# Two causal attentions of one Trainium2 kernel: from batches of whole heads to units of four heads and half the queries

## The reference, cut to what matters

```python
# layer 0: queries and keys get a bias and a rotation by position
q, k, v = (x @ W + b for each).reshape(16 heads, 16)
# gate of layer 1's feed-forward part: the same without bias and rotation
scores = einsum('bqhd,bkhd->bhqk', q, k) / sqrt(16)
scores = where(k_index <= q_index, scores, -large)
out = softmax(scores) @ v        # then a product with Wo
```

## Time and profile before

| what | us |
|---|---|
| median of three runs | 3222.04 |
| lowest, highest | 3208.08, 3231.48 |
| the profiled execution's own time | 3223.99 |
| its span, first to last instruction | 3222.1 |
| TensorE busy in the span | 2691.4 |
| VectorE busy | 1827.7 |
| GpSimd busy | 1411.9 |
| ScalarE busy | 1229.2 |
| first attention in the span, first transfer to last multiplication | 60.05 to 319.64 |
| second attention, the same | 1580.76 to 1838.22 |
| mean granted TensorE clock, share of full speed | 0.895 |

### The profile page before, as it was taken

The page is one execution under the profiler, slowest core; times in us unless marked ns, Lnnn a source line. Parts: engine busy times, 40 slices in busy tenths (PEclk is TensorE's granted clock), DMA queues, the critical chain, the costliest instruction groups (busy, mean ns, idle before and its releaser), DMA issues. The chain is left out here.

```text
span 3222.1 us, 41641 instructions
## 1 busy us (share of the span) xinstructions
PE 2691.4 (84%) x13826; PEld 1822.3 (57%) x13826; DVE 1827.7 (57%) x2624; ACT 1229.2 (38%) x2035; POOL 1411.9 (44%) x1110
## 2 busy tenths in 40 slices
PE   4888799767999999998588876868787777998798
PEld 3454677543444444445444455756676665776676
DVE  3753355456666666633366233676757576554465
ACT  4355233353555555552345422323232332233222
POOL 2542334364888888882255122313131221343133
PEclk7789899897999999998678888889989987998799
DMA  1310111121111111100121011001000000110011
GB/s 52 49 21 1 39 44 44 41 69 40 34 33 34 27 27 27 27 1 26 29 43 21 7 42 39 24 1 34 0 26 8 21 7 21 34 49 28 21 35 42
DMA packets 47269, 94.03 MB, mean 29 GB/s; under 512 B 11553, under 2 KB 25761, under 8 KB 46497
## 3 DMA queue, kind: packets, MB, share of 16 engines
q1 hardware_dynamic: 44544, 88.53, 11.2%
q10 hardware_dynamic: 2592, 3.82, 0.3%
HBM read 59.81 MB, written 3.15 MB: 20 GB/s over the span
## 5 line engine op out<-in xcount | busy, mean ns | idle before, releaser
L2042 DVE TENSOR_REDUCE a1h_mseg<-bank 128x2 f32<-128x1024 f32 x256 | 302.4, 1222 | 185.2 <-PE bank L1807 177.0
L1969 ACT ACTIVATE a1h_prob<-bank 128x512 f32<-128x512 f32 x440 | 247.3, 598 | 190.8 <-PE bank L1863 105.0
L1791 POOL TENSOR_TENSOR a_qk<-a_qk,a1h_prob 128x512 f32<-128x512 f32 x230 | 298.4, 1332 | 49.1 <-ACT a1h_prob L1969 49.0
L63 POOL TENSOR_TENSOR f_wh<-f_raw,ones_r 128x768 fp32r<-128x768 f32 (+1 forms) x74 | 111.3, 1504 | 406.4 <-PE bank L402 371.9
L391 PE MATMUL bank<-x_norm_h,f_wh 128*128 128x512 f32 x592 | 242.2, 409 | 10.6 <-POOL f_wl L359 10.1
L391 PE MATMUL bank<-x_norm_l,f_wh 128*128 128x512 f32 x592 | 237.4, 401 | 0.0
L391 PE MATMUL bank<-x_norm_h,f_wl 128*128 128x512 f32 x592 | 236.7, 400 | 0.0
L600 DVE SCALAR_TENSOR_TENSOR f_tf<-bank,f_bias,f_sg 128x512 f32<-128x512 f32 x148 | 111.0, 751 | 202.6 <-PE bank L391 181.7
L2425 POOL TENSOR_TENSOR x_norm<-x_norm,l2a_tab 128x512 f32<-128x512 f32 x64 | 87.9, 1381 | 298.0 <-ACT x_norm L2639 247.7
L1876 PE MATMUL bank<-a1h_prob,a_v 128*64 128x512 f32 x880 | 215.0, 603 | 0.0
L1861 PE MATMUL bank<-a1h_ql,a1h_k 128*128 128x512 f32 x512 | 202.0, 395 | 0.0
(11 more groups left out here) (581 smaller groups left out, 6996.8 us busy)
## 6 DMA issues: line engine op xcount, KB each, us to landing
f_raw<-in_l_w_dram SPq DMA_DIRECT2D x66, 385.0 KB, 3.1
a1h_st_q<-a_qk SPq DMA_DIRECT2D x128, 128.0 KB
a_staging<-a_qk SPq DMA_DIRECT2D x384, 32.0 KB
a_qk<-l_keys SPq DMA_DIRECT2D x32, 128.0 KB, 2.7
l2a_vraw<-in_l2a_wvg_dram SPq DMA_DIRECT2D x8, 512.0 KB, 4.1
l2a_qkraw<-in_l2a_wqk_dram SPq DMA_DIRECT2D x32, 128.0 KB, 2.1
f_raw<-in_l_w_dram SPq DMA_DIRECT2D x8, 449.0 KB, 3.4
a1p_raw<-in_l1a_w_dram SPq DMA_DIRECT2D x20, 128.0 KB, 2.0
```

The source lines that it names most:

```text
L63: return pool.tensor_tensor(dst, src, one.to_broadcast(list(src.shape)), ALU.mult)
L1791: pool.tensor_tensor(out, first, slot_of[t % NP], ALU.add).then_inc(sum_done, 1)
L1969: act.activation(slot_of[t % NP], core.bank[2 + t % 3][:, :], ACT.Exp, scale=scale).then_inc(p_ready, 1)
L2042: dve.tensor_reduce(mseg[:, :, qb, s], spare(("A", n, k))[:, :, :], AX.X, ALU.max).then_inc(a_read, 1)
```

## The change

Only the two causal attentions, and what feeds them, are touched. `attend` and `attend_plan` are taken out; `attend_causal` takes their place.

- The work is cut into 8 units: four heads ("quad" Q) and one half h of the queries. A unit of the first half has 4 steps of 128 keys, one of the second half 8, so 48 steps in all. Order: (0,0) (1,0) (0,1) (1,1) (2,0) (3,0) (2,1) (3,1).
- A head's operand has 64 rows: high, low and high parts in 16 rows each, and 16 rows for the maxima. Two heads lie in one 128-row tile; their products are issued side by side in the upper and the lower 64 rows of the array.
- Rows are gathered by transfers of 64 KB, 12 for two heads (96 instead of 192 in all). They read the high and low parts, which are now made once for all heads on the four source chunks, before the gather. ScalarE copies the gathered rows into operands of type fp32r (`rounding`), 16 copies of 128x1024; the first eight stand ahead of all exponentials in its order.
- Maxima: 48 visits of 4 products each, two reductions of 128x2 by up to 1024 columns. Visits run up to 11 ahead of the steps. The maxima of a unit go to rows by 8 fp32 products with a negated identity, and VectorE adds them to the query rows. GpSimd does nothing in the loop.
- Scores go to three banks in turn instead of two. Masks are products of 64 rows by 64 columns, two for each head instead of one of 128x128.
- Values: as before four column tiles, now read straight from `v` (the copies at L1519 go).
- A unit's end works on 512 columns instead of 1024; ScalarE spreads the inverse, and results overwrite the query chunk Q in place.
- The zero and one fills of `a_staging` (second and third fill, L987) go; two fills of 128x2048 are made inside the new block. Weights' order and constants are laid out to match.

```diff
-    HEADS = 8
-    per = 4 if causal else 2
...
+def attend_causal(nc, core, name, qk, v, scale, masks_dram):
+    QUADS = 4
+    UNITS = [(2 * g + b, h) for g in range(2) for h in range(NH) for b in range(2)]
+    KEYS_OF = (4, 8)
+    K = 64
+    NP = 12
+    SLOTS = 3
...
+    def visits_by(g):
+        return min(len(visits), 6 + g + 1 + min(4, max(0, g - 1)))
+    head = [("A", x) for x in range(4)] + [("M", 0)] + [("A", x) for x in range(4, 6)]
...
+    for w in range(len(UNITS)):
+        after[LAST_STEP[w] + 3].append(("D", w))
+        after[LAST_STEP[w] + 5].append(("R", w))
...
+        @block.sync
+            for i in range(2 * QUADS):
+                g, j0 = i // 4, 2 * (i % 4)
+                if i == 0:
+                    sp.wait_ge(filled, 2)
+                for c in range(2):
+                    if i >= 2:
+                        sp.wait_ge(rounded, 2 * (i - 2) + c + 1)
+                    part = ((HI, 0), (HI, 16), (LO, 32)) if c == 0 else ((HI, 0), (HI, 32), (LO, 16))
+                    for src, r in part:
+                        sp.wait_ge(hi if src is HI else lo[g], ...)
+                        for u in range(2):
+                            sp.dma_start(raw[c][64 * u + r:64 * u + r + 16, i % 2, :],
+                                         src[g][j0 + u:P:8, c, :].bitcast(F32)).then_inc(rows_in[i % 2][c], 16)
...
+            def maxima(x):
+                if h == 0 and qb == 0:
+                    pe.wait_ge(rounded, 4 * (Q + 1))
+                for p in range(2):
+                    wait_spare(pe, ("A", x, p))
+                    for u in range(2):
+                        rows = slice(64 * u, 64 * u + K)
+                        mm = pe.matmul(ps[:, u, 0:n], qt[rows, ..., qb * P:(qb + 1) * P],
+                                       kt[rows, ..., s * HALF:s * HALF + n], ..., tile_position=(64 * u, 0))
...
+            def max_rows(w):
+                for i in range(8):
+                    mm = pe.matmul(ps[:, i // 4, (i % 4) * P:(i % 4 + 1) * P], mpos[:, w % 2, i, :], nident[:, :],
+                                   start=True, stop=True)
...
+            def scores(g):
+                for p in range(2):
+                    for u in range(2):
+                        t = 4 * g + 2 * p + u
+                        if t >= 3:
+                            pe.wait_ge(p_ready, t - 2)
+                        mm = pe.matmul(core.bank[2 + t % 3][:, 0:n], kt[...], qt[...], ..., tile_position=(64 * u, 0))
+                    if diag:
+                        for c in range(2):
+                            for u in range(2):
+                                mm = mask(pe, core.bank[2 + t % 3][:, 64 * c:64 * c + 64], 1, c, u)
...
+            def values(g):
+                for b in range(4):
+                    mm = pe.matmul(core.bank[5][32 * b:32 * b + 32, c0:HALF], v[:, kb, 4 * Q + b, :],
+                                   prob[:, (4 * g + b) % NP, 0:n], ..., tile_position=(0, 32 * b))
...
+            for g in range(len(steps) + 6):
+                if g < len(steps):
+                    scores(g)
+                others([e for e in after[g] if e[0] in "AM"])
+                if 0 < g <= len(steps):
+                    values(g - 1)
+                others([e for e in after[g] if e[0] in "DR"])
...
+            high(0)
+            high(1)
+            for i in range(4):
+                for c in range(2):
+                    rounding(i, c)
...
+                    for b in range(4):
+                        act.wait_ge(s_ready, t + 1)
+                        act.activation(prob[:, t % NP, 0:n], core.bank[2 + t % 3][:, 0:n], ACT.Exp, scale=scale)
...
+                    dve.tensor_reduce(mseg[:, w % 2, 2 * p:2 * p + 2, qb % 4, s], spare(("A", x, p))[:, :, 0:n], AX.X,
+                                      ALU.max).then_inc(a_read, 1)
...
 def small_attention(nc, core, name, a, key, on, dst, tables, v_bias, add_x):
-        attend(nc, core, name + "h", qk, 2, None, v, on, 0.25, True, 2, a["spread"], a["causal"], staging=staging)
+        attend_causal(nc, core, name + "h", on, v, 0.25, a["causal"])
```

More of the change, by code:

```diff
@@ new lines, in values @@
+            def values(g):
+                w, kb = steps[g]
+                Q, h = UNITS[w]
+                c0, n, diag = width(g)
+                if kb == 0 and w:
+                    pe.wait_ge(ou_done, w)
+                pe.wait_ge(p_ready, 4 * g + 4)
+                for b in range(4):
+                    mm = pe.matmul(core.bank[5][32 * b:32 * b + 32, c0:HALF], v[:, kb, 4 * Q + b, :],
+                                   prob[:, (4 * g + b) % NP, 0:n], start=kb == 0, stop=kb == KEYS_OF[h] - 1,
+                                   skip_group_check=True, tile_position=(0, 32 * b))
+                mm.then_inc(av_done, 1)
@@ new lines, in sums, with inverse @@
+            def sums(w):
+                wait_spare(pe, ("D", w))
+                pe.wait_ge(ou_done, w + 1)
+                ps = spare(("D", w))
+                for b in range(4):
+                    mm = pe.matmul(ps[:, 0, 4 * b:4 * b + 4], ou[:, w % 2, b * P:(b + 1) * P], pick[:, :], start=True,
+                                   stop=True)
+                mm.then_inc(a_ready, 1)
+            def inverse(w):
+                wait_spare(pe, ("R", w))
+                pe.wait_ge(rx_done, w + 1)
+                ps = spare(("R", w))
+                for b in range(4):
+                    mm = pe.transpose(ps[:, 0, b * P:(b + 1) * P], rx[:, b, :, :].rearrange("p a d -> p (a d)"),
+                                      core.ident[:, :])
+                mm.then_inc(a_ready, 1)
@@ new lines, in others @@
+            def others(events):
+                for kind, x in events:
+                    if kind == "A":
+                        maxima(x)
+                    elif kind == "M":
+                        max_rows(x)
+                    elif kind == "D":
+                        sums(x)
+                    else:
+                        inverse(x)
+            pe.wait_ge(made, 3)
+            others(head)
+            for g in range(len(steps) + 6):
[5 more added lines that the diff above has]
+                others([e for e in after[g] if e[0] in "DR"])
@@ new lines, in scale_products @@
+            def scale_products(w):
+                Q, h = UNITS[w]
+                dve.wait_ge(a_ready, use["R", w] + 1)
+                dve.wait_ge(ou_done, w + 1)
+                dve.tensor_tensor(qk[:, Q, half(h)], ou[:, w % 2, :], spare(("R", w))[:, 0, :],
+                                  ALU.mult).then_inc(on_done, 1)
+            dve.wait_ge(made, 3)
+            for kind, x in head:
+                if kind == "A":
+                    maxima(x)
+                else:
+                    add_maxima(x)
@@ new lines, in _ @@
+            for g in range(len(steps) + 6):
+                for kind, x in [e for e in after[g] if e[0] in "AM"] + [e for e in after[g] if e[0] in "DR"]:
+                    if kind == "A":
+                        maxima(x)
+                    elif kind == "M":
+                        add_maxima(x)
+                    elif kind == "D":
+                        invert(x)
+                    elif kind == "R":
+                        scale_products(x)
+            dve.wait_ge(on_done, len(UNITS))
```

737 lines of the change are left out of this document (205 added, 532 removed).

## The result

| | us |
|---|---|
| forecast (range) | 3169 (3080 to 3240) |
| kernel after, median of four runs | 3270.98 (3258.84 to 3290.16) |
| kernel before, measured beside it | 3224.16 (3208.08 to 3231.48) |
| ratio after/before, with its 95% interval | 1.0144 (1.011 to 1.0178) |
| profiled execution after: time, span, mean clock | 3269.16, 3267.3, 0.869 |

The change made the kernel slower by 1.4%, and the time lies outside the range. What came is close to the price of the third rival ("the clock stays low", 3280), but 20 of the 45 us lie in a block that this rival does not speak of.

The account below looks back on a forecast made before the run. In the attention loops TensorE's stream binds for three batches, the score-to-exponential chain in the last. Gains 2 x (17.5 start + 6.2 loop + 2.1 end) + 1 = 52.6 us give 3171.4, with the lower median 3169 us; range 3080 to 3240.

Parts of the forecast that it names:

- third rival: Attention loops: the clock stays low; at two thirds low the loop takes 244 us, the kernel 3280; chance 0.11.
- Start: Each attention's start: first exponential at 99.7 us, about 40 behind the block's start instead of 57; gain 17.5 us.
- the rival of a gather bound by rate: Attention start: transfers run at 48.7 GB/s, first exponential 15 us later than before, kernel 3235 us; chance 0.09.
- The loop's work: Each attention's loop at full clock: steps, visits, maxima, sums, transposes and waits add up to 178.7 us.
- The chain of a step: Loop: fourth score waits for the first's exponential, since three banks turn; 2.61 us for a full step without visit.
- second rival: Attention loops: two heads' products don't run side by side; 23 us more, 212 with the clock, kernel 3217; chance 0.11.
- The clock: Attention loops: 13% at the low clock, half the old share, makes 178.7 into 188.5 us; gain 6.2.
- The progress at the low clock: Loop at 1.2 GHz: a step with a visit goes from 3.2 to 5.3 us, progress 0.6.
- The prediction's own bounds for the loop: Loop gain: 16 us with no low clock, −49 with two thirds low.
- The first rival: Attention loops: waits overlap better, TensorE's own 122.6 us binds, 131 with low clock; kernel 3055 us; chance 0.25.
- The end: Each attention's end, from last values to multiplication: 5.65 us instead of 7.8, gain 2.1.
- Other stages: Stages outside the two attentions: taken as unmoved; the forecast would be wrong if they move by over 3 us.

Follow-up runs that it names:

- the ninth: Kernel after with four extra 64-row products of 512 columns, two and two side by side, ahead of each visit half: 3256.2 us, ratio 1.011.
- the second experiment: Kernel after with a unit's maxima moved to rows by 8 transposes instead of 8 fp32 products, VectorE subtracting them: 3266.8 us, ratio 1.0145.
- the best kernel: Kernel after with the visit between the score pairs, maxima as transposes and 65 idle TensorE instructions more in each causal attention: 3140.2 us, ratio 0.9745.
- 12: Kernel after with 104 instructions (waits already met) more in TensorE's program of each causal attention: 3265.6 us, ratio 1.0134.
- 13: Kernel after with the visit between the score pairs, maxima as transposes and 97 idle TensorE instructions more in each causal attention: 3157.2 us, ratio 0.9794.
- 15: Kernel after with the visit between the score pairs, maxima as transposes and a padding of 481 TensorE instructions in each causal attention: 3227.3 us, ratio 1.002.
- The third experiment: Kernel after with a step's maxima visit between its two score pairs, or the values of the step before where there is no visit: 3173.5 us, ratio 0.9875.
- the eighth: Kernel after with the visit split, one half behind each pair of scores, then the values: 3196.8 us, ratio 0.9923.
- 17: Kernel after with 76 instructions (waits already met) more in TensorE's program of each causal attention: 3258.7 us, ratio 1.0105.

## Why the prediction was wrong

**Start: right in sum.** Forecast 40 us from block start to first exponential, 40 measured. The price per transfer was 0.62 us where I had 0.67, and the scores behind the copies took 2.0 us that I had at nothing; that the two cancel is luck. The gain was 17 us of the 17.5; the rival of a gather bound by rate is out.

**The loop's work: right within a tenth, on the high side.** Forecast 178.7 us at full clock. By the full-clock stretch TensorE is busy 29.79/36 = 83%, and its work is 135 us, so 163; the ninth's second loop, all at full clock, less 47 us of extra products gives the same. The forecast "TensorE busy for 70 to 75%" was too low accordingly. The chain of a step came as forecast: full steps without a visit are 2.66 us apart at full clock (forecast 2.6), and 4.12 at the low one. Side by side products work (second rival out).

**The clock: the step that failed.** The text said: "Unit ends are now half as long each, so I take half of the old share, 13%". Measured: 60%, and 64% in the second loop. At 13% the work of 163 us would have taken some 173; at 60% it took 226. That is −53 us in the first attention and −57 in the second, where the whole gain forecast was 52.6. Of the 98 us between forecast and profile the two loops make 79 (226.0 and 230.0 against 188.5) and the state attention 20. Two things in that sentence were wrong. The low clock does not come from the unit ends: the second experiment shortened them, and the share did not fall (80% in its profile). And the old share was no property that carries over: a new stream of instructions has a clock of its own. The progress at the low clock, which I had at 0.6, was well sized: 163 us at full clock and 135 x 2.1/0.93 = 305 at the low one give 0.53.

The forecast gave this rival 0.11, with break-even at a share of 0.41. The rows of before spoke for it more loudly than I read them: the earlier trace rows showed full clock with TensorE 79% busy and the low clock with it 100% busy, so busy time explains nothing, and no row showed a stream like the new one. The prediction's own bounds for the loop, +16 to −49 us, hold the −31 and −37 measured; the point that it took between them was a guess.

**The first rival ("the waits overlap better")** needed TensorE's own work, 122.6 us, to bind. The work was 135 us and TensorE was idle for another 29. With the visit between the pairs idle time is still 22 us of 176, and the best kernel took 3140 us, not 3055.

Two side sums of the prediction are off, and neither enters the forecast: 122.6 us with 13% at the low clock give 129 and not 131, and 0.625 us per transfer with short fills gives a gain of 23 at the start and not 20.

**The end: half of it,** 1.1 us of 2.1, since the sums ran at the low clock.

**Other stages: the second failure.** The forecast took them as unmoved and named 3 us as the point from which it would be wrong. They moved by 20 us, through the place of a loop in TensorE's program. The Trainium skill (Runtime: NRT & Kernel Launch, Instruction fetch mechanics) says that a taken branch whose target isn't in the current window of two pages has to fetch it before it goes on. The trace agrees with the fetch: packets on the instruction queue and a wait of 5 us come and go together. It does not agree with two pages of 256 instructions for TensorE: in the kernel before, the loop of 1746 instructions repeats three times with 7 packets over the whole state attention and no such wait. The same section has 2048 instructions for TensorE in blocks of 256; the paddings worked out with that block length (12, 13 and 15) missed, so the measurement does not bear out its use for choosing a place.

The parts sum to the result. First attention: start +17.4, the removed fills +3.3 (the block starts at 56.7 instead of 60.05), end +1.1, loop −31.3, together −9.5; the first product behind it came 9.4 us later. Second attention: start +18.4, fills +1.3, end +0.9, loop −37.4, together −16.8. The stages between lost 0.5. With −20.1 in the state attention that is −47, of which the rest of the kernel gives back 2.

## What to carry to other kernels

Read TensorE's clock as a term of its own and don't carry it over: bound it from 0 to the whole loop when the order or the kind of products changes, and try two or three orders of the same products, since here one cost 97 us less than another with the same instructions. When a change alters the number of instructions ahead of a long hardware loop, compare the packets of the instruction queue and the "issue" waits at each pass; a few idle instructions can be worth 20 us. And compare the blocks that were not touched before explaining those that were.

## What the runs showed of the hardware

- TensorE stood at 1.2 GHz for 36 us on end while busy for 93% of the time, and at 2.4 GHz for 36 us while busy for 83%. At 1.2 GHz its work took twice as long (s = 2.1), and a step with waits in it 4.12 us instead of 2.66.
- The clock of a loop followed the mix and order of products: 0.60 with transposes for fp32 products (one profile, of the longest of its runs), 0.70 as written, 0.88 with the visit moved, 0.87 with full rows, 0.95 and 1.00 with 192 pairs of thin products more. Adding work made a loop 19 us shorter. Neither idle time (18 us of 191 at 0.78, 28 of 219 at 0.95) nor width orders all ten kernels. What the chip goes by stays open. The Trainium skill (TensorE: Matmul & The Clock Gate, A second HAM failure mode: psum-queue depth-cycling) says of another kernel that short idle times between groups of products make the clock fall and rise again and again. The third experiment goes that way (idle 29 to 22 us, clock 0.70 to 0.88), the eighth and ninth do not.
- A pair of 64-row products of 512 columns side by side costs 0.28 us at full clock (47 us for 168 pairs; 0.57 for two in a row). The forecast had taken 0.29 from a row. The Trainium skill (TensorEngine Tiling, Theoretical Speedup) says up to 2x, from which the prediction's estimate was 0.43 us for two pairs; the 0.57 measured does not reach it.
- A hardware loop of 1746 instructions on TensorE repeats without a wait at one place of the program (0.8 us of idle time) and with a wait of 5 us a pass at another, with 9 packets of 16 KB fetched each time; in between only some passes pay (one of three with 17, where 8 packets more were fetched).
- Between the profiles of four kernels with the same attention code the two loops together varied by 17 us at the same idle time, so through the clock. The runs of one kernel spread by 0.2 to 1%, up to 31 us (3258.84 to 3290.16 for the kernel after, clock 0.873 to 0.857), so this can be scatter from run to run as well. A difference of 10 us between two kernels of this kind needs a look at each loop's clock, and more than one run, before it is put down to the edit.
